# Graph attention score passes: five identity products on TensorE ahead of each group's score transposes

## The chip, the cores and the metric

The kernel runs on one core of a Trainium2 chip. Its time is the device time of one execution in microseconds (us), taken without a profiler; the median of three runs stands for it. The profile comes from one further execution under the hardware profiler, which is longer than the timed runs: its span is 4777.7 us.

## The reference, cut to what matters

Two layers over 3125 nodes and 50000 edges. Layer 0 is a weighted neighbour sum with a small MLP and a mixture of experts. Layer 1 begins with a typed graph attention, then a slice attention. The change touches only the scores of the graph attention:

```
K, Q, V = typed linear maps of the node rows
att   = einsum('ehd,ed->eh', k, q.sum(heads)) / sqrt(56)      # edges src -> dst, k from src, q from dst
att_i = the same with src and dst exchanged
att, att_i = softmax over the edges that end in one node
agg   = sum of att * v over those edges, both directions
```

`k` is the K row of one end with a time embedding behind it, `q` the Q row of the other end summed over four heads (56 numbers, also with a time embedding). A softmax over segments needs the maximum of each segment first, so each direction takes a score pass (all scores, and maxima) and a sum pass (exponentials and weighted sums).

## The kernel before, in words

The edges are sorted by the node in which they end and laid out in 416 blocks of 128 slots, each block in one window of 128 nodes. Four blocks are a group (U = 4), 104 groups are a pass (NG = 104). For each direction `o` there is `score_*(o)` and then `sum_*(o)`, one function for each engine; all loops are written out, each engine runs its instructions in order, and semaphores tie them together.

A group of a score pass goes as follows.

- **GpSimd** (POOL, L1349) gathers the K and V rows of the group's 512 edges with four indirect DMAs into one of four buffers; SyncE loads the edges' time embeddings beside them (L1311) and writes the V rows out for the sum pass (L1326).
- **ScalarE** (ACT) makes the one-hot matrices of the group: `onehot` with four Abs (L1504) and one Relu (L1506). Its other functions are `turned` and `masks`, which copy the turned one-hots out of PSUM bank 0 (L1514 and L1519), and `scores`, which copies the turned score terms out of bank 1 (L1526) and the scores themselves (L1527). In 26 of the 104 steps of a pass it also clears a tile of the accumulator (`clear`, L1530).
- **TensorE** (PE) has four functions: `turn` transposes the four one-hots into bank 0 (L1441); `queries` fetches the summed Q rows into bank 2 or 3, in turn (L1454, L1457 and L1459); `turn_att` transposes the score terms of the group into bank 1 (L1469); `spread` spreads the scores over the nodes of the window in banks 4 to 7, with a mask (L1478 and L1480, four of each, in two halves).
- **VectorE** (DVE) multiplies the K rows with the query bank (L1393, semaphore `prod`), sums to scores (L1400), splits these into three bf16 terms (L1405 to L1408, semaphore `att` after the last), and takes the maxima of the banks 4 to 7 in two halves (L1380, semaphore `bmr`), one half before and one after the split.

TensorE's order is fixed by the loop at L1484. In step `s` it runs `turn_att(s+1)`, `spread(s)`, `queries(s+3)`, `turn(s+4)`. ScalarE's step has `scores(s+1)`, `clear` in each fourth step, `turned(s+3)`, `onehot(s+4)`, `masks(s+3)`. VectorE's step has the product of group `s+2`, its sums, the first maxima of group `s`, the split of group `s+2`, and the second maxima of group `s`.

The waits that matter here: `turn_att(g)` waits for `att` of group g. `scores(g)` on ScalarE waits for `turn_att(g)`. `turn(g+3)`, which needs bank 0 free, waits for `masks(g+2)`, the last thing of ScalarE's step. `queries(g)` waits for the product of group g-2, since this frees the query bank. The second half of `spread(g)` waits for the second maxima of group g-1.

`identb` is a bf16 identity of 128x128.

Of the kernel before, what the change touches and what calls it, by code (L numbers as in the profile page):

```python
# [15 lines left out]
P = 128  # L16
# [9 lines left out]
NG = NB // U  # L26
# [24 lines left out]
def build(nc, A, out):  # L51
    ctx = ExitStack()
    with ctx:
# [3 lines left out]
        def sem(name):  # L57
            if name not in sems:
                sems[name] = ctx.enter_context(nc.semaphore(name))
            return sems[name]  # L60

        def sb(name, shape, dt=F32):
            return ctx.enter_context(nc.sbuf_tensor(name, shape, dt))
# [28 lines left out]
        identb = sb("identb", [P, P], BF16)  # L92
# [33 lines left out]
        PS = [PSA[:, 512 * k:512 * (k + 1)] for k in range(8)]  # L126
# [39 lines left out]
        def loads_of(eng, ap_row, maxv, etype):  # L166
            _, vals = nc.values_load_multi_w_load_instructions(
                ap_row, engines=[etype], min_val=0, max_val=maxv,
                skip_runtime_bounds_check_because="clamped when the table was computed")
            return vals  # L170
# [1127 lines left out]
        def halves(x):  # L1298
            return x.bitcast(BF16).rearrange("p (j two) -> p j two", two=2)[:, :, 1]
# [53 lines left out]
        def score_vector(ve, o):  # L1353
# [67 lines left out]
            ins.then_inc(sem("pass_set"), 1)  # L1421
            ve.drain()

        OT2 = [PS[s][:, 0:U * P // 2].bitcast(BF16) for s in range(2)]

        def transposes(pe, s):
            for u in range(U):
                ins = pe.transpose(OT2[s % 2][:, u * P:(u + 1) * P], halves(OH[s][:, u, :]), identb[:, :])  # L1428
            return ins
# [4 lines left out]
        def score_tensor(pe, o):  # L1434
            def turn(g):
                G = o * NG + g
                pe.wait_ge(sem("oh"), G + 1)
                if g:
                    pe.wait_ge(sem("ot"), 2 * G)
                for u in range(U):  # L1440
                    ins = pe.transpose(OHP[:, u * P:(u + 1) * P], OHB[g % SL][:, u, :], identb[:, :])  # L1441
                ins.then_inc(sem("ohT"), 1)

            def queries(g):
                G, s = o * NG + g, g % SL
                if G == 0:
                    pe.wait_ge(sem("kv_tab"), 32)
                ws = loads_of(pe, win[o][0:1, g * U:(g + 1) * U], W - 1, ET.PE)
                pe.wait_ge(sem("ot"), 2 * G + 1)
                pe.wait_ge(sem(f"edges{s}"), 16 * (3 * o * (NG // SL) + g // SL + 1))  # L1450
                if g >= 2:
                    pe.wait_ge(sem("prod"), G - 1)
                q = PS[2 + g % 2][:, 0:U * 64].rearrange("p (u c) -> p u c", c=64)
                pe.matmul(PS[2 + g % 2][:, 0:U * 64], ZB, identb[:, :].unsqueeze(1).to_broadcast([P, U * 64 // P, P]),  # L1454
                          start=True, stop=False, skip_group_check=True)
                for u in range(U):
                    pe.matmul(q[:, u, 0:DK], OTF[g % 2][:, u, :], QS[:, ds(ws[u], 1), :].rearrange("p t d -> p (t d)"),  # L1457
                              start=False, stop=False, skip_group_check=True)
                pe.matmul(q[:, :, DK - TD:DK], ident[:, :], KVR[s][:, :, KV + 2 * TD:ROW],  # L1459
                          start=False, stop=True, skip_group_check=True).then_inc(sem("q"), 1)  # L1460

            def turn_att(g):
                G = o * NG + g
                pe.wait_ge(sem("att"), G + 1)
                if g:
                    pe.wait_ge(sem("tb"), 2 * G - 1)
                b = BF[g % 2].rearrange("p k n -> p (k n)").bitcast(BF16).rearrange("p (r x) -> p r x", x=2 * H1)
                for h in range(H1):
                    ins = pe.transpose(ATP[0:NR, h * P:(h + 1) * P], b[:, :, 2 * h + 1], identb[:, :])  # L1469
                ins.then_inc(sem("att_t"), 1)  # L1470

            def spread(g):
                G = o * NG + g
                pe.wait_ge(sem("tb"), 2 * G + 1)
                for u in range(U):
                    if u % 2 == 0 and g:
                        pe.wait_ge(sem("bmr"), 2 * (G - 1) + u // 2 + 1)
                    pe.matmul(PS[4 + u], identb[:, :], NEG[g % SL][:, u, :].unsqueeze(1).to_broadcast([P, H1, P]),  # L1478
                              start=True, stop=False, skip_group_check=True)
                    ins = pe.matmul(PS[4 + u], SEL[:, u, :], ATB[g % 2], start=False, stop=True, skip_group_check=True)  # L1480
                    if u % 2:
                        ins.then_inc(sem("bm"), 1)

            for step in range(-4, NG):  # L1484
                if 0 <= step + 1 < NG:
                    turn_att(step + 1)
                if step >= 0:
                    spread(step)
                if 0 <= step + 3 < NG:
                    queries(step + 3)  # L1490
                if step + 4 < NG:
                    turn(step + 4)
# [168 lines left out]
        def sum_scalar(act, o):  # L1661
            def copies(g):
                G = o * NG + g
                act.wait_ge(sem("oh2T"), G + 1)
                if g >= 2:
                    act.wait_ge(sem("m"), G - 1)
                act.activation(OT[g % 2].rearrange("p u n -> p (u n)"), OT2[g % 2], ACT.Copy).then_inc(sem("ot2"), 1)

# [796 lines left out]
        @block.tensor  # L2465
        def _(pe):
            rank_tensor(pe, 0)
            rank_tensor(pe, 1)
            place_tensor(pe, "t", OHt.rearrange("p t g -> p (t g)"), T1)
            l0_tensor(pe)  # L2470
            mlp_tensor(pe)
            route_tensor(pe)
            experts_tensor(pe)
            kvq_tensor(pe)
            for o in range(2):
                score_tensor(pe, o)
                sum_tensor(pe, o)
            slice_prep_tensor(pe)
            turn_types(pe)
            proj_tensor(pe)  # L2480
            gamma_tensor(pe)
            slices_tensor(pe)
            tokens_tensor(pe)
            final_tensor(pe)
# [63 lines left out]
```

## Time and profile before

| | us |
|---|---|
| median of three timed runs | 3957.93 (3956.56 to 3957.97) |
| span of the profiled execution, its own time | 4777.7 |
| score pass, first direction (2260.1 to 2972.3 of the span) | 712.2 |
| score pass, second direction (3339.3 to 4037.7) | 698.4 |

Busy over the whole profiled span: PE 2872.2 us (60%), DVE 2426.9 (51%), ACT 1720.4 (36%), POOL 2723.8 (57%). Times in the rows below are in us from the start of the span. "Granted clock" is the share of TensorE's full 2.4 GHz that its throttle let through: 1.00 or 0.50 (1.2 GHz), and values between the two are means over a stretch. Under the profiler the program takes 819.8 us longer than without it, so a stall seen in the rows need not be in the timed runs.

### The profile page before, as it was taken

What the parts mean: (1) busy time and instruction counts of PE and PEld (TensorE: products, weight loads), DVE (VectorE), ACT (ScalarE), POOL (GpSimd) and SP (SyncE); (2) the same over time, 40 slices, a digit from 0 to 9 for tenths busy, and PEclk for the clock granted to TensorE, in tenths of its full rate; (3) what the DMA queues carried; (4) which work ended last, traced back from release to release, by engine and by line L of the source; (5) the groups of instructions that cost most, each with busy time, mean ns of one, the idle gap of its engine ahead of it and who ended that gap; (6) DMA issues with size and microseconds to landing.
All of it is one profiled execution on the core that took longest, in us unless ns stands there. A gap on an engine that the chain in (4) does not pass through costs nothing.

```text
span 4777.7 us, 52094 instructions
## 1 busy us (share of the span) xinstructions
PE 2872.2 (60%) x13590; PEld 1938.9 (41%) x13692; DVE 2426.9 (51%) x4965; ACT 1720.4 (36%) x4345; POOL 2723.8 (57%) x2661
## 2 busy tenths in 40 slices
PE   3200025555533239367677777997777776997588
PEld 1000013333332126223444444887444444886445
DVE  7444444544421001433667677566677777566353
ACT  2232300000011002222455554786555554885451
POOL 5676756666645740466555554788555553555551
PEclk6555557767665569767777777999777777998799
DMA  4343356333414224267766667687777666665300
GB/s 143 113 172 126 143 111 231 89 89 91 98 57 165 97 89 148 68 200 212 216 199 208 200 200 184 177 213 184 205 202 209 201 202 166 160 173 149 110 1 27
DMA packets 767484, 720.00 MB, mean 151 GB/s; under 512 B 389089, under 2 KB 661163, under 8 KB 767068
## 3 DMA queue, kind: packets, MB, share of 16 engines
q1 hardware_dynamic: 645116, 399.08, 29.2%
q0 software_dynamic: 115136, 314.24, 22.4%
q10 hardware_dynamic: 6944, 3.34, 0.2%
q8 instruction: 119, 1.95, 0.2%
q14 instruction: 169, 1.38, 0.1%
HBM read 482.09 MB, written 243.22 MB: 152 GB/s over the span
## 4 chain that ended last, share of the span: by engine, by line
PE 22%; another core or an unknown queue 17%; DVE 16%; issue 12%; ACT 9%; DVEq 4%; POOL 2%; ACTq 2%; DMA 1%; SPq 1%; POOLq 0%
DVE META L1380 5%; DVE BIGR L605 3%; ACT AR L1674 3%; DVE AR L1400 3%; PE ps L1657 2%; PE ps L933 2%; PE ps L944 2%; ACT AR L1676 2%; DVE AR L596 2%; DVEq L1396 2%; PE ps L1480 1%; PE ps L1478 1%; ACTq L1675 1%; PE ps L1428 1%
## 5 line engine op out<-in xcount | busy, mean ns | idle before, releaser
L1349 POOL DMA_INDIRECT AR<-kv_tab,META x832 | 793.7, 954 | 620.8 <-DVE AR L1393 363.1
L1380 DVE TENSOR_REDUCE META<-ps 128x8 f32<-128x1024 f32 x416 | 508.5, 1223 | 186.3 <-remote 94.2
L493 POOL DMA_INDIRECT rec_dst<-AR,slot_e x400 | 403.3, 1008 | 229.1 <-issue 171.0
L625 PE MATMUL ps<-AR 128*128 128x256 f32 x832 | 318.2, 550 | 345.4 <-DVE AR L596 156.4
L579 POOL DMA_INDIRECT AR<-xn_tab,META x416 | 398.6, 958 | 206.8 <-issue 139.0
L1618 POOL TENSOR_TENSOR AR<-AR 128x896 f32<-128x896 f32 x208 | 351.4, 1689 | 246.1 <-ACT AR L1683 241.6
L1583 DVE TENSOR_TENSOR BIGR<-BIGR,ps 128x260 f32 x832 | 354.3, 426 | 217.4 <-PE ps L1657 131.1
L1478 PE MATMUL ps<-AR,identb 128*128 128x512 bf16 x832 | 403.8, 485 | 79.1 <-issue 55.2
L1657 PE MATMUL ps<-AR 128*128 128x260 f32 x1664 | 413.9, 392 | 2.1 <-POOL AR L1618 2.0
L625 PEld LDWEIGHTS ps<-AR 128*128 128x128 f32 x832 | 219.7, 277 | 445.1 <-issue 214.9
L1526 ACT ACTIVATE AR<-ps 12x512 bf16<-12x512 bf16 x208 | 122.1, 587 | 671.8 <-remote 469.9
L521 POOL DMA_INDIRECT rec_src<-AR,slot_e x290 | 286.6, 988 | 97.5 <-issue 93.1
L1480 PE MATMUL ps<-AR 128*128 128x512 bf16 x730 | 340.9, 467 | 0.0
L605 DVE TENSOR_TENSOR BIGR<-BIGR,ps 128x256 f32 x416 | 174.8, 420 | 311.3 <-remote 151.4
L1393 DVE TENSOR_TENSOR AR<-AR,ps 128x896 f32<-128x896 f32 x208 | 225.2, 1083 | 196.8 <-remote 174.1
L1657 PEld LDWEIGHTS ps<-AR 128*128 128x128 f32 x1664 | 302.0, 192 | 41.1 <-POOL AR L1618 3.3
L1457 PEld LDWEIGHTS ps<-QS,AR 128*128 128x128 f32 x1664 | 271.0, 247 | 19.8 <-issue 12.4
L1457 PE MATMUL ps<-QS,AR 128*128 x1664 | 278.2, 325 | 0.0
L1674 ACT ACTIVATE AR<-iota,META 128x128 f32<-128x128 f32 x832 | 263.4, 390 | 28.3 <-DVE AR L1420 28.3
L1504 ACT ACTIVATE AR<-iota,META 128x128 f32<-128x128 f32 x832 | 262.3, 385 | 24.6 <-DVE AR L1370 24.6
L749 ACT ACTIVATE AR<-ps 128x256 f32<-128x256 f32 x25 | 9.6, 383 | 686.0 <-PE ps L706 663.2
L1400 DVE TENSOR_REDUCE AR<-AR 128x16 f32<-128x896 f32 x208 | 225.9, 1086 | 34.3 <-issue 33.5
(430 smaller groups left out, 5624.0 us busy)
## 6 DMA issues: line engine op xcount, KB each, us to landing
v_dst<-AR SPq DMA_DIRECT2D x104, 384.0 KB
AR<-v_dst SPq DMA_DIRECT2D x104, 384.0 KB
v_src<-AR SPq DMA_DIRECT2D x104, 384.0 KB
AR<-v_src SPq DMA_DIRECT2D x104, 384.0 KB
AR<-in_W_qvk SPq DMA_DIRECT2D x44, 608.0 KB
rec_raw<-AR SPq DMA_DIRECT2D x40, 640.0 KB
AR<-rec_dst SPq DMA_DIRECT2D x104, 192.0 KB
AR<-rec_src SPq DMA_DIRECT2D x104, 192.0 KB
```

What stands on the lines that cost most here:

```text
L493: pool.indirect_dma_start(rec_tab[0], bass.IndirectOffsetOnAxis(ap=slot_e[0][:, c * CC + k:c * CC + k + 1].bitcast(U32), axis=0), RD[s][0] ...
L579: pool.indirect_dma_start(GA[s][:, u, :], None, xn_tab, bass.IndirectOffsetOnAxis(ap=META[0][:, g * U + u, 0:1].bitcast(U32), axis=0)).the ...
L625: ins = pe.matmul(l0_ps(s, u), OW[s][:, u, :], GA[s][:, u, :], start=True, stop=True)
L1349: pool.indirect_dma_start(KVR[s][:, u, 0:KV], None, kv_tab, bass.IndirectOffsetOnAxis(ap=META[o][:, g * U + u, 0:1].bitcast(U32), axis=0)) ...
L1380: ve.tensor_reduce(BMALL[o][:, g * U + 2 * half:g * U + 2 * half + 2, :].rearrange("p b h -> p (b h)"), PSA[:, 2048 + 1024 * half:3072 + 1 ...
L1400: ve.tensor_reduce(x, PRD.rearrange("p u (h d) -> p (u h) d", d=DK), AX.X, ALU.add)
L1457: pe.matmul(q[:, u, 0:DK], OTF[g % 2][:, u, :], QS[:, ds(ws[u], 1), :].rearrange("p t d -> p (t d)"), start=False, stop=False, skip_group_ ...
L1478: pe.matmul(PS[4 + u], identb[:, :], NEG[g % SL][:, u, :].unsqueeze(1).to_broadcast([P, H1, P]), start=True, stop=False, skip_group_check= ...
L1480: ins = pe.matmul(PS[4 + u], SEL[:, u, :], ATB[g % 2], start=False, stop=True, skip_group_check=True)
L1583: ve.tensor_tensor(a, a, PS[4 + u][:, 0:SROW], ALU.add).then_inc(sem("add"), 1)
L1657: pe.matmul(PS[4 + u][:, 0:SROW], OH[s][:, u, :], VB[s][:, u, :], start=True, stop=True).then_inc(sem("sum"), 1)
L1674: act.activation(DIST2[g % 2][:, u, :], iota1[:, :], ACT.Abs, scale=-1.0, bias=META[o][:, g * U + u, 1:2])
```

## The change

At the head of TensorE's step stands a new wait and five matrix products of `identb` with itself, repeated to 512 columns. They are written to the query bank that `queries(step + 3)` fills later in the same step; this first overwrites the bank (`start=True`). The wait is for the product of group `step + 1`, the one that reads this bank last. It happens in the steps 0 to 100 of each pass, that is 202 times, and adds 1010 matrix products.

```
@@ score passes, TensorE @@
+        def warm(pe, bank, width, times):
+            for _ in range(times):
+                pe.matmul(bank[:, 0:width], identb[:, :], identb[:, :].unsqueeze(1).to_broadcast([P, width // P, P]),
+                          start=True, stop=True, skip_group_check=True)
...
             for step in range(-4, NG):
+                if 1 <= step + 1 < NG and step + 3 < NG:
+                    pe.wait_ge(sem("prod"), o * NG + step + 2)
+                    warm(pe, PS[2 + (step + 3) % 2], 512, 5)
                 if 0 <= step + 1 < NG:
                     turn_att(step + 1)
```

## Rows read from the trace of the kernel before

**Rows 1.** The page: granted clock of TensorE in 40 equal slices of the span.

```profile
PEclk6555557767665569767777777999777777998799
```

**Rows 2.** Stretches: both score passes, then one sum pass; columns as named in the first line.

```profile
core 0: us, PE busy (x) PEld busy (x) DVE busy (x) ACT busy (x) POOL busy (x), PEclk, DMA share, GB/s
2260.10:2972.30 712.20, 521.54 (x2722) 318.72 (x2771) 496.56 (x718) 362.04 (x948) 390.16 (x409) 0.75 0.69 203
3339.30:4037.70 698.40, 509.38 (x2718) 311.75 (x2769) 496.79 (x718) 362.02 (x948) 380.94 (x402) 0.77 0.72 201
3003.40:3318.00 314.60, 307.28 (x2043) 274.02 (x2042) 192.19 (x513) 251.39 (x704) 275.72 (x208) 1.00 0.77 201
```

**Rows 3.** Timeline of one group without a stall: start, duration, engine, line.

```profile
2618.69 1.23 DVE L1380 TENSOR_REDUCE META<-ps 128x8 f32<-128x1024 f32 x1
2619.01 0.39 PE L1441 MATMUL ps<-identb,AR 128*128 128x128 bf16 x4
2619.32 0.40 PE L1469 MATMUL ps<-identb,AR 128*12 128x128 bf16 x4
2619.76 0.59 ACT L1526 ACTIVATE AR<-ps 12x512 bf16<-12x512 bf16 x1 [1.39 <-PE ps L1469]
2619.83 1.08 DVE L1393 TENSOR_TENSOR AR<-AR,ps 128x896 f32<-128x896 f32 x1
...
2620.10 0.38 PE L1478 MATMUL ps<-AR,identb 128*128 128x512 bf16 x1
2620.32 0.38 PE L1480 MATMUL ps<-AR 128*128 128x512 bf16 x1
2620.36 0.57 ACT L1514 ACTIVATE AR<-ps 128x512 f32<-128x512 bf16 x1
2620.82 0.96 POOL L1349 DMA_INDIRECT AR<-kv_tab,META  x1 [0.30 <-issue]
2620.84 1.26 ACT L1504 ACTIVATE AR<-iota,META 128x128 f32<-128x128 f32 x4
...
2622.17 0.63 ACT L1506 ACTIVATE AR<-AR 128x512 bf16<-128x512 f32 x1
2622.34 0.45 PE L1459 MATMUL ps<-AR,ident 128*128 128x128 f32 x2
2622.71 0.58 ACT L1519 ACTIVATE AR<-ps 128x512 bf16<-128x512 bf16 x1
2623.43 0.38 PE L1441 MATMUL ps<-identb,AR 128*128 128x128 bf16 x4 [0.65 <-ACT AR L1519]
2623.70 0.18 DVE L1408 TENSOR_TENSOR AR<-AR 128x16 bf16<-128x16 f32 x1
2623.80 1.22 DVE L1380 TENSOR_REDUCE META<-ps 128x8 f32<-128x1024 f32 x1
2623.94 0.40 PE L1469 MATMUL ps<-identb,AR 128*12 128x128 bf16 x4
```

**Rows 4.** The instructions of L1530: times run, duration in ns min/median/max, first and last start.

```profile
L1530 ACT ACTIVATE BIGR<-ones x52: 401/401/403, 2284.3 to 4031.5; 128x260 f32<-128x260 f32 x52
```

**Rows 5.** Stretches without a stall, columns as in rows 2: clock and TensorE's busy time.

```profile
2617.70:2621.10 3.40, 3.40 (x27) 2.35 (x26) 3.17 (x7) 2.01 (x6) 1.24 (x2) 1.00 0.82 272
2965.90:2969.30 3.40, 2.83 (x18) 1.87 (x17) 3.17 (x4) 1.82 (x5) 0.00 (x0) 1.00 0.25 81
```

**Rows 6.** A stretch at the low clock, columns as in rows 2.

```profile
2600.60:2604.00 3.40, 3.18 (x11) 1.26 (x11) 3.17 (x4) 2.82 (x8) 2.74 (x3) 0.50 0.60 168
```

**Rows 7.** Timeline around a stall: low clock before, and low clock again behind it.

```profile
2602.69 0.63 PE L1478 MATMUL ps<-AR,identb 128*128 128x512 bf16 x1
2603.11 0.63 PE L1480 MATMUL ps<-AR 128*128 128x512 bf16 x1
...
2608.09 1.22 DVE L1380 TENSOR_REDUCE META<-ps 128x8 f32<-128x1024 f32 x1 [2.77 <-issue]
2609.72 0.59 ACT L1526 ACTIVATE AR<-ps 12x512 bf16<-12x512 bf16 x1 [5.09 <-remote]
2611.14 1.86 PE L1457 MATMUL ps<-QS,AR 128*128 x8
```

## The prediction

> **What bounds the kernel now.** I read the page's slices first. TensorE's granted clock is 9 tenths or more only in the two short stretches where it is also busiest, and 6 to 7 tenths in most of the rest [rows 1]. Then I set the four passes of the graph attention side by side. A score pass takes 712.2 or 698.4 us at a mean clock of 0.75 to 0.77, a sum pass some 315 us at 1.00 [rows 2]. So the score passes are 1410.6 us of the profiled span of 4777.7 us, 6.8 us for each of 208 groups, and none of the four engines is busy all of it. This is the place that the change touches, and the low clock there is what it could cure.
>
> Next I read the timeline of a group, and there are two kinds. In a group without a stall VectorE is never idle: from the second maxima of one group (2618.69) to those of the next (2623.80) are 5.11 us, filled by the product, the sums, two maxima and the split [rows 3]. I call its period 5.10 us. GpSimd issues a gather every 0.96 + 0.30 us, four of which are 5.04 us, so it is close behind [rows 3]. In the other kind something holds the core for about 3 us: VectorE begins its maxima 2.77 us late with nothing named, ScalarE its copy after 5.09 us idle [rows 7]. At 5.10 us each, the 208 groups would take 1061 us, so stalls make up 350 us of the two passes. The profiled execution is 819.8 us longer than the timed runs. I take it that the stalls belong mostly to the profiler's execution, and that the timed kernel runs its score passes near 5.10 us a group. It is an assumption, and two of the rivals drop it.
>
> **What the low clock costs now.** At the low clock [rows 6] the wide products of `spread` start 0.42 us apart and the eight of L1457 take 1.86 us [rows 7]; at the high clock the wide ones start 0.22 us apart [rows 3], half of it. In the groups without a stall the clock is at its high level [rows 5] although TensorE is busy for only 2.83 of 3.40 us. So without stalls the kernel keeps the high clock by itself, and even right after a stall, where it is low, TensorE sits behind VectorE's 5.10 us by little. What the change can buy back is therefore near nothing.
>
> The Trainium skill speaks for the change: "TensorE: Matmul & The Clock Gate", section "Why this matters for your kernels", advises to leave no long idle gaps between bursts of matmuls, since the clock then falls to half. The trace agrees that the clock is low beside the stalls and high away from them; what filling would bring if the rule decided here is the third rival.
>
> **What the change adds, step by step.**
>
> *Products.* Five bf16 products of 512 columns. The same shape is L1478 and L1480, which start 2620.32 - 2620.10 = 0.22 us apart at the high clock; over the eight of a group it is 0.215. Five are 1.08 us. At the low clock they start 0.42 us apart [rows 7], and five are 2.1 us.
>
> *The wait.* It is for the product of group g that `turn_att(g)` needs anyway through `att`, 3.0 us later: L1393 ends at 2620.91, L1408 at 2623.88 [rows 3]. The wait by itself holds nothing that `turn_att` would not hold. I cost it at 0; between 0 and one semaphore instruction a group, which is under 0.1 us.
>
> *Is TensorE's idle time the cover?* By its busy time, yes: the group's own work is 3.02 us from 2619.32 to 2622.34, then L1459's 0.45 and L1441's 0.31 (2619.01 to 2619.32), at most 3.8 us of 5.10 [rows 3]. With 1.08 more it is 4.9. But the idle time lies in the wrong place. TensorE idles before `turn`, since bank 0 is not free until ScalarE's last copy (L1441 waited 0.65 us for L1519). The new products stand behind `turn` and ahead of `turn_att`, where hardly 0.30 us is idle (2623.43 + 0.31 to 2623.94, and that is the wait for `att`).
>
> *The loop that they lengthen.* `turn_att` starts ScalarE's step, ScalarE's step ends with `masks`, `masks` frees bank 0 for `turn`, and `turn` stands ahead of the next `turn_att` on TensorE. Its parts from start to start [rows 3]: L1469 to L1526 0.44; L1526 to L1514 0.60; L1514 to L1504 0.48; L1504 to L1506 1.33; L1506 to L1519 0.54; L1519 to L1441 0.72; L1441 to the next instruction of TensorE 0.31. The sum is 4.42 us. Now it is hidden behind VectorE's 5.10, with 0.68 to spare. With the products between `turn` and `turn_att` it is 4.42 + 1.08 = 5.50 us, and it takes the lead. A clear (L1530) of 0.40 us stands in it in every fourth step [rows 4], which was hidden as well: 0.10 a group more, 5.60 us.
>
> *Sum.* 5.60 - 5.10 = 0.50 us for each of 202 groups is 101 us. Nothing hides it: VectorE then waits for the first half of `spread`, and the gathers' 5.04 us and what the DMA needs fit in with room. Everything outside the score passes stays. Bounds of this term: if only what exceeds VectorE's period counts and no clear adds, 0.40 x 202 = 81 us; if the wait and the first product's start add 0.1, 121 us.
>
> The sum against the profiled execution is 4777.7 + 101 = 4879, with more if products fall into the low clock beside a stall. Carried to the timed runs, which lack 819.8 us of it, it is **3957.9 + 101 = 4059 us**.
>
> **The rivals.**
>
> *1. Cover from elsewhere.* Score groups of the timed runs already take longer than 5.10 us because of DMA. For it: the 16 DMA engines are busy for 0.69 of 712.2 us [rows 2], that is 4.7 us of each group, and the gathers' issue takes 5.04. Against: groups at 5.10 occur while gathers run. At a true period of 5.4 the price is 0.2 x 202 = 40 us, at 5.6 nothing: 3958 to 3998, say 3975.
>
> *2. The stalls are in the timed runs too.* Then ScalarE's copy, late behind `turn_att` by the stall, is on the same loop, and the stall leaves the low clock, so that the five cost 2.1 in one group and 1.08 in the next, with 0.2 to 0.3 us of slack in each: (2.1 + 1.08 - 0.5)/2 = 1.3 us a group at the most, 0.7 if the clock stays up. 202 groups give 140 to 275 us: 4100 to 4230. Against: then the 819.8 us must come from the rest of the program alone.
>
> *3. Faster: the clock decides.* If the timed kernel runs its score groups at 1.2 GHz, TensorE's group is at least 3.8 + 8 x 0.21 for `spread` + 0.8 for L1457 (1.86 less what half of that leaves, with its own 0.1 of start) = 6.3 us and is itself the bound. Were that so in half of the groups, a mean group takes 5.7 us. With the five it takes 5.6, and the kernel is 20 us faster; were it so in all, 6.3 to 5.6 saves 140 us: 3818 to 3938, say 3900. It decides only where the low clock is found in more than 0.5/1.2 = 42% of the groups. For it: the mean of 0.75, which is half the time at the low level. Against: the low level stands beside the stalls, and the group right behind one is VectorE's again.
>
> **How the numbers follow.** The loop through ScalarE, 4059 us with its own range 4035 to 4085, gets 0.58. The covered case (3975) gets 0.17, the stalls that stay (4100 to 4230) 0.12, the clock (3900) 0.13. About 0.2% (8 us) is what a measurement of this kernel can tell from no change. The clock's case is faster by more than that: with a little for luck, faster 0.13. Of the covered case somewhat over half falls within 8 us: same 0.10. The rest is slower: 0.77. For 8 in 10 I leave out the faster case below 3950 and the upper part of the stalls' above 4125.
>
> **What the changed profile would show.** If the step is right: five new products between L1441 and L1469 in each group; L1469 late behind L1408 by 0.5 us or more; groups without a stall at 5.5 to 5.6 us; VectorE idle before its first maxima, with TensorE's spread as what ended it; ScalarE idle for some 2 us ahead of its L1526 and hardly elsewhere. The granted clock of the score passes would rise from 0.75 without their time falling. Rival 1 shows groups no longer than before, L1469 still released by VectorE. Rival 3 shows shorter score passes. I am wrong if `turn` ends well before `att` in the undisturbed groups, for then the five lie in idle time.

## The result and the profile after

The changed kernel takes 4046.01 us (median of four, 4042.42 to 4049.05), the kernel before 3957.95 (median of four, 3956.56 to 3958.45): 88 us slower, ratio 1.0223 with a 95% interval of 1.0211 to 1.0235. The forecast was 4059 us.

The profiled execution of the changed kernel has a span of 4044.2 us and a device time of 4045.93, in the middle of the other three. A profiled execution is therefore not bound to be longer, and the 4777.7 us of the profile before need another reason than the profiler. The runs below show one. They come in two conditions: in one the kernel before takes 3957 us, in the other it takes 4742 to 4772 us (medians on three chips), with the stalls of [rows 7] in its traces. I call the second the condition with stalls. Each price below is against the kernel before on the same chip and in the same condition. Two executions that fit neither condition, one of the kernel before (4372.71 us) and one of a changed kernel (6208.72 us), are left out of the ratios, which can differ in the fourth place from those of the medians.

The page of the kernel after: span and instructions, then the granted clock in 40 slices.

```profile
span 4044.2 us, 54114 instructions
...
PEclk6555557777776996889999989998999999997798
```

Stretches of the kernel after, columns as in [rows 2]: its two score passes, then its first sum pass.

```profile
1805.50:2378.30 572.80, 496.11 (x3221) 295.86 (x3271) 488.80 (x718) 361.34 (x947) 389.08 (x409) 0.99 0.86 253
2745.00:3317.10 572.10, 495.69 (x3221) 295.80 (x3270) 489.75 (x718) 361.38 (x947) 380.77 (x403) 0.99 0.89 246
...
2410.30:2725.00 314.70, 307.47 (x2044) 274.69 (x2043) 192.25 (x513) 251.51 (x704) 275.54 (x208) 1.00 0.77 201
```

The clock of the score passes is 0.99, and each takes 572 us. [Rows 2] have 0.75 and 0.77, but from the condition with stalls, so the two clocks alone do not say what the products did to it. From product to product there are 103 steps in a pass, 5.56 us each. VectorE is busy for 488.8 of 572.8 us: it waits. The sum pass is as before, 314.7 us.

Timeline of one group of the kernel after, which answers to [rows 3]. Lines have moved: L1427 is the new product; L1475, L1535, L1523, L1513, L1515, L1528 and L1447 are what L1469, L1526, L1514, L1504, L1506, L1519 and L1441 were.

```profile
2100.84 0.40 PE L1475 MATMUL ps<-identb,AR 128*12 128x128 bf16 x4
...
2101.28 0.59 ACT L1535 ACTIVATE AR<-ps 12x512 bf16<-12x512 bf16 x1 [1.98 <-PE ps L1475]
...
2101.88 0.57 ACT L1523 ACTIVATE AR<-ps 128x512 f32<-128x512 bf16 x1
...
2102.26 1.23 DVE L1380 TENSOR_REDUCE META<-ps 128x8 f32<-128x1024 f32 x1 [0.48 <-PE ps L1486]
...
2102.36 1.26 ACT L1513 ACTIVATE AR<-iota,META 128x128 f32<-128x128 f32 x4
...
2103.69 0.63 ACT L1515 ACTIVATE AR<-AR 128x512 bf16<-128x512 f32 x1
2103.72 0.18 DVE L1408 TENSOR_TENSOR AR<-AR 128x16 bf16<-128x16 f32 x1
...
2104.22 0.58 ACT L1528 ACTIVATE AR<-ps 128x512 bf16<-128x512 bf16 x1
2104.95 0.38 PE L1447 MATMUL ps<-identb,AR 128*128 128x128 bf16 x4 [0.64 <-ACT AR L1528]
...
2105.17 1.24 PE L1427 MATMUL ps<-identb 128*128 128x512 bf16 x5
...
2106.34 0.40 PE L1475 MATMUL ps<-identb,AR 128*12 128x128 bf16 x4
```

Read it as a loop, from L1475 to L1475. To ScalarE's first copy 0.44 us, then 0.60, 0.48, 1.33, 0.53 along ScalarE's step, 0.73 to `turn`, 0.22 to the first product, and 1.17 through the products to the next `turn_att`. (A start here is that of the first instruction of each kind.) The sum is 5.50 us, and the group lasts 5.50 us. From `turn` to the instruction behind it are 0.22 us, less than the 0.31 before the change, so the new wait holds nothing. `att` (L1408, done at 2103.90) has been ready for 2.4 us when `turn_att` starts at 2106.34: VectorE no longer sets the pace. ScalarE waits 1.98 us for `turn_att`, VectorE 0.48 us for the spread scores.

The same over all groups, from the page's costliest groups: ScalarE's wait for `turn_att` in both passes.

```profile
L1535 ACT ACTIVATE AR<-ps 12x512 bf16<-12x512 bf16 x208 | 121.9, 586 | 415.4 <-PE ps L1475 415.4
```

That is 2.0 us for each of 208 groups. A group with a clear shows the second part, here ScalarE's timeline with and then without it:

```profile
2084.49 0.59 ACT L1535 ACTIVATE AR<-ps 12x512 bf16<-12x512 bf16 x1 [1.98 <-PE ps L1475]
2084.98 0.20 ACT L1536 ACTIVATE AR<-AR 128x16 f32<-128x16 f32 x1
2085.09 0.40 ACT L1539 ACTIVATE BIGR<-ones 128x260 f32<-128x260 f32 x1
2085.39 0.57 ACT L1523 ACTIVATE AR<-ps 128x512 f32<-128x512 bf16 x1
...
2090.29 0.59 ACT L1535 ACTIVATE AR<-ps 12x512 bf16<-12x512 bf16 x1 [1.98 <-PE ps L1475]
2090.79 0.20 ACT L1536 ACTIVATE AR<-AR 128x16 f32<-128x16 f32 x1
2090.89 0.57 ACT L1523 ACTIVATE AR<-ps 128x512 f32<-128x512 bf16 x1
```

From L1535 to L1523 are 0.90 us with the clear and 0.60 without: the copies and the clear overlap by 0.1, and the clear costs 0.30 of its 0.40.

### The profile page after: what moved, and what is told of

The parts are those of the page before. It is cut to its first block, busy times and chain, and to the rows that moved or that the text cites. A ratio compares the mean times of both kernels' runs of the same rounds, so it can differ in the third digit from the quotient of the medians.

```text
span 4044.2 us, 54114 instructions
## 1 busy us (share of the span) xinstructions
PE 2752.9 (68%) x14600; PEld 1872.6 (46%) x14702; DVE 2419.8 (60%) x4965; ACT 1719.1 (43%) x4345; POOL 2730.1 (68%) x2661
## 4 chain that ended last, share of the span: by engine, by line
PE 30%; ACT 20%; issue 15%; DVE 5%; POOL 5%; ACTq 4%; DMA 4%; DVEq 1%; SPq 1%; POOLq 1%
PE ps L625 6%; ACT AR L1513 6%; PE ps L1427 5%; ACT AR L1683 5%; ACT AR L1528 3%; PE ps L944 3%; ACT AR L1685 3%; ACT AR L1523 2%; ACTq L1514 2%; PE ps L1447 2%; ACTq L1684 2%; PE ps L1434 2%; PE ps L1475 2%; PE ps L933 1%; DMA BIGR<-in_L_ffn_w 1%
## 5 line engine op out<-in xcount | busy, mean ns | idle before, releaser
L625 PE MATMUL ps<-AR 128*128 128x256 f32 x832 | 303.6, 530 | 287.5 <-issue 216.4
L625 PEld LDWEIGHTS ps<-AR 128*128 128x128 f32 x832 | 210.5, 265 | 381.5 <-issue 340.1
L1484 PE MATMUL ps<-AR,identb 128*128 128x512 bf16 x832 | 320.0, 385 | 5.9 <-DVE META L1380 0.5
L1666 PEld LDWEIGHTS ps<-AR 128*128 128x128 f32 x1664 | 302.6, 192 | 40.4 <-POOL AR L1627 3.2
L1535 ACT ACTIVATE AR<-ps 12x512 bf16<-12x512 bf16 x208 | 121.9, 586 | 415.4 <-PE ps L1475 415.4
L1486 PE MATMUL ps<-AR 128*128 128x512 bf16 x730 | 279.0, 382 | 0.0
L1513 ACT ACTIVATE AR<-iota,META 128x128 f32<-128x128 f32 x832 | 262.2, 385 | 24.6 <-DVE AR L1370 24.6
L1427 PE MATMUL ps<-identb 128*128 128x512 bf16 x1010 | 252.8, 382 | 0.0
```

What stands on the lines that cost most here:

```text
L625: ins = pe.matmul(l0_ps(s, u), OW[s][:, u, :], GA[s][:, u, :], start=True, stop=True)
L1427: pe.matmul(bank[:, 0:width], identb[:, :], identb[:, :].unsqueeze(1).to_broadcast([P, width // P, P]), start=True, stop=True, skip_group_ ...
L1513: act.activation(DIST[:, u, :], iota1[:, :], ACT.Abs, scale=-1.0, bias=META[o][:, g * U + u, 1:2])
L1666: pe.matmul(PS[4 + u][:, 0:SROW], OH[s][:, u, :], VB[s][:, u, :], start=True, stop=True).then_inc(sem("sum"), 1)
```

## The experiments

The theory is the loop: the products stand between `turn` and the next `turn_att`, and that chain through ScalarE becomes longer than VectorE's 5.10 us. Its rivals here are that five more products cost what they cost wherever they stand, that the new wait costs, and that the clock decides.

**The place.** The wait and the five products are moved to just before `queries`. The kernel ran in both conditions; the run without stalls, the later one, is shown first.

```diff
             for step in range(-4, NG):
-                if 1 <= step + 1 < NG and step + 3 < NG:
-                    pe.wait_ge(sem("prod"), o * NG + step + 2)
-                    warm(pe, PS[2 + (step + 3) % 2], 512, 5)
                 if 0 <= step + 1 < NG:
                     turn_att(step + 1)
                 if step >= 0:
                     spread(step)
+                if 1 <= step + 1 < NG and step + 3 < NG:
+                    pe.wait_ge(sem("prod"), o * NG + step + 2)
+                    warm(pe, PS[2 + (step + 3) % 2], 512, 5)
                 if 0 <= step + 3 < NG:
                     queries(step + 3)
```

> The five products between spread and queries once more, for a run where the kernel before takes 3958 us. Loop theory there: TensorE's chain is 4.4 + 0.31 = 4.7 us, under VectorE's 5.10: 3958 to 3973 us. Rival, TensorE's plain time or traffic: 4046 us. Where stalls of 3 us come in every other group and the kernel before takes some 4742 us: 10 us more than before, as measured.

Measured, without stalls: 3961.07 us against 3956.59 for the kernel before, ratio 1.0011 (1.0002 to 1.0020). The same 1010 products and the same 202 waits cost 88 us in one place and 4 us in the other, as the loop had it (3958 to 3973) and not its rival (4046). Its timeline, one group:

```profile
2033.37 1.22 DVE L1380 TENSOR_REDUCE META<-ps 128x8 f32<-128x1024 f32 x1
2033.52 0.41 PE L1475 MATMUL ps<-identb,AR 128*12 128x128 bf16 x4 [0.33 <-DVE AR L1408]
...
2035.59 1.24 PE L1427 MATMUL ps<-identb 128*128 128x512 bf16 x5
...
2036.90 0.58 ACT L1528 ACTIVATE AR<-ps 128x512 bf16<-128x512 bf16 x1
...
2037.90 0.39 PE L1447 MATMUL ps<-identb,AR 128*128 128x128 bf16 x4
...
2038.47 1.22 DVE L1380 TENSOR_REDUCE META<-ps 128x8 f32<-128x1024 f32 x1
2038.61 0.40 PE L1475 MATMUL ps<-identb,AR 128*12 128x128 bf16 x4 [0.33 <-DVE AR L1408]
```

The group lasts 5.10 us from maxima to maxima, and `turn_att` is released by VectorE's L1408. Here `turn` (2037.90) comes behind TensorE's own queue, 0.4 us after bank 0 was free, and there are still 0.33 us to spare. Its two score passes:

```profile
1805.50:2339.70 534.20, 492.35 (x3268) 303.58 (x3267) 489.89 (x718) 361.10 (x946) 388.97 (x409) 0.98 0.92 271
2706.20:3232.20 526.00, 491.21 (x3273) 302.39 (x3271) 488.91 (x717) 361.64 (x948) 381.00 (x403) 0.99 0.95 268
```

Together 1060.2 us, against 1144.9 for the changed kernel. The difference, 84.7 us, is all but 1 us of that between the two spans (4044.2 and 3958.5). So the whole loss lies in the score passes and in the place of the products. Clock and TensorE's busy time are alike in both (0.98 to 0.99; 983.6 and 991.8 us), which leaves neither the clock nor plain TensorE time as the cause. The moved kernel also tells against the case in which the clock decides: its passes run at the high clock, nearly all their groups last 5.10 us, and it isn't faster than before.

The kernel before has no trace without stalls, but its executions beside the moved kernel have a mean clock each. The median is 0.833, against 0.839 for the moved kernel. If the whole difference lies in the score passes, which are 1060 of 3958 us, then those of the kernel before run at about 0.96, by my estimate; at 0.76 its mean would have been some 0.78. So without stalls there was hardly any clock to win back.

The same kernel with stalls:

> The same wait and the same five products, moved from the head of the step to between spread and queries, so that they no longer stand between turn and the next turn_att. Loop theory: TensorE's chain from turn_att to turn is 3.3 + 1.08 = 4.4 us and ScalarE's 4.1, then 0.31 for turn, together 4.7 under VectorE's 5.10: 3958 us, up to 15 more. Rival, plain TensorE time or traffic (five more products cost what they cost wherever they stand): 4046 us. Rival, the clock: 3900 us, since the clock is high and the loop is not lengthened.

4753.25 us against 4741.99, ratio 1.0026 (1.0016 to 1.0036), 11 us. The values expected were for 3958 us and are not tested by it.

**The wait alone**, with stalls: the change without its five products.

```diff
                 if 1 <= step + 1 < NG and step + 3 < NG:
                     pe.wait_ge(sem("prod"), o * NG + step + 2)
-                    warm(pe, PS[2 + (step + 3) % 2], 512, 5)
```

> Only the wait for the product, without the five products. Loop theory: the wait is met 3 us before turn_att's own, so 3958 us, within 8 us of before. Rival, the wait: the time of the changed kernel, about 4046 us, or a good part of it.

4743.93 against 4741.99 us, ratio 1.0001 (0.9990 to 1.0012). No price of the wait shows in this condition. In the other it was not run alone; there the timeline after has products right behind `turn`, 0.22 us after its start.

**The condition with stalls.** The kernel before, unchanged, was profiled twice more, each time for a trace without stalls.

> The kernel before, unchanged, profiled a second time, to see its score passes without the profiler's stalls. Loop theory (the five products lengthen the chain turn, products, turn_att, ScalarE's step, turn): a span near 3956 us, both score passes together about 1058 us, groups of 5.10 us with VectorE never idle, and TensorE's clock at 0.9 to 1.0 in them. Rival, the clock: the clock in these passes is near 0.75 here too, and groups are uneven.

> The kernel before once more, profiled, hoping for an execution without stalls (3957 us). Loop theory: every group of both score passes 5.10 us, VectorE busy all of it, both passes together some 1058 us, and TensorE's clock at 0.9 to 1.0 in them, so that there was nothing for the filler to cure. Rival, the clock: near 0.75 there even without stalls.

Both fell into the condition with stalls: 4742.22 us (ratio 1.0003, 0.9992 to 1.0014) and 4774.14 us (0.9997, 0.9982 to 1.0012). So there is no trace of the kernel before without stalls, and the group of 5.10 us in it, with VectorE never idle, rests on [rows 3] and on the moved kernel. These are the score passes of the first of the two.

```profile
2255.50:2949.90 694.40, 516.14 (x2768) 313.72 (x2767) 493.17 (x717) 361.56 (x948) 388.95 (x409) 0.76 0.71 208
3317.90:4000.00 682.10, 518.02 (x2764) 312.78 (x2765) 493.90 (x718) 361.56 (x948) 379.85 (x402) 0.77 0.76 206
```

The low mean clock of 0.76 belongs to this condition, and so do the 6.7 us a group. The score passes hold less than half of the loss: in the profile before they take 350 us more than in the moved kernel's trace (1410.6 against 1060.2), and the part ahead of them takes 455 us more (2260 against 1805.5). The sum pass has none of it. The runs with stalls were on three chips and those beside the moved kernel without stalls on a fourth, so it stays open whether the condition goes with the chip or with the time, and what the stalls are; no run here tells it.

**The change in that condition.**

> The changed kernel once more. Where the kernel before takes 3958 us: 4046 us. Where it takes some 4742 us, with stalls of about 3 us in every other group of the score passes: loop theory, if a stall lies on the loop turn, products, turn_att, ScalarE's step: 0.45 to 1.3 us a group more, 4830 to 5000 us. Rival, the stall runs beside the products and covers them in every other group: the five cost half or less, 4745 to 4790 us.

4769.19 us against 4744.75, ratio 1.0052 (1.0033 to 1.0070), 24 us. This is the rival's value (4745 to 4790); what the loop theory expected here, 4830 to 5000, is missed. The interval also overlaps that of the moved kernel with stalls (11 us), so in this condition the place of the products is not shown to matter. Its score passes:

```profile
2244.00:2946.40 702.40, 549.50 (x3273) 309.22 (x3271) 494.86 (x718) 361.50 (x947) 388.83 (x409) 0.91 0.70 206
3317.30:4014.10 696.80, 551.40 (x3270) 311.04 (x3270) 495.54 (x718) 361.62 (x948) 379.81 (x402) 0.92 0.73 202
```

The clock rose from 0.76 to 0.91 and the passes did not get shorter: 1399.2 us against 1376.5, the latter from another chip; a second trace of the kernel before with stalls has 1403.2. VectorE's products in the changed kernel, over two groups:

```profile
2559.07 1.09 DVE L1393 TENSOR_TENSOR AR<-AR,ps 128x896 f32<-128x896 f32 x1 [3.00 <-remote]
...
2564.18 1.08 DVE L1393 TENSOR_TENSOR AR<-AR,ps 128x896 f32<-128x896 f32 x1
...
2572.39 1.09 DVE L1393 TENSOR_TENSOR AR<-AR,ps 128x896 f32<-128x896 f32 x1 [1.61 <-remote]
```

One group lasts 5.11 us and the next 8.21, together 13.32 (`remote` stands for a release by another core or an unknown queue). Of the 206 steps of both passes 95 last about 5.10, although the loop with the products needs 5.50, and such a pair has a median of 13.33 us, where the kernel before has 13.30 to 13.45 in its traces with stalls. Two turns of the lengthened loop, 11.0 us at the high clock, fit into that. So what the loop adds disappears in time that the stall takes anyway, in most pairs; where the 24 us lie is not shown.

**The number of products**, three and ten in place of five, at the place of the change.

```diff
-                    warm(pe, PS[2 + (step + 3) % 2], 512, 5)
+                    warm(pe, PS[2 + (step + 3) % 2], 512, 3)      # the other kernel: 10
```

> Three products in place of five, in the place of the change. Loop theory: 4.42 + 3 x 0.215 = 5.07 us, just under VectorE's 5.10; only the groups with a clear (one in four) go over, by about 0.3 us: 3958 + 50 x 0.3 = 3973 us. Rival, cost in proportion to the products: 3958 + 88 x 3/5 = 4011 us.

> Three products at the place of the change. Without stalls, loop theory: 4.42 + 0.65 = 5.07 us, under VectorE's 5.10, over it only in groups with a clear: 3957 + 50 x 0.3 = 3972 us. Rival, in proportion to the products: 4010 us.

> Ten products in place of five, same place. Loop theory where no stalls are: each product beyond the third adds its 0.215 us to each of 202 groups, so 5 more than the changed kernel add 217 us: 4263 us, a group 6.6 us. Where stalls are: 150 to 220 us more than the changed kernel. Rival, TensorE's own busy time is the bound: 3.8 + 2.15 = 5.9 us a group, 4120 us.

> Ten products at the place of the change. Without stalls, loop theory: 5.50 + 5 x 0.215 = 6.6 us a group, 4046 + 217 = 4263 us. Rival, TensorE's busy time as the bound: 3.8 + 2.15 = 5.9 us a group, 4120 us.

All four ran with stalls, so the values expected for 3957 us were not tested. Three cost 6 us (4748.08 against 4741.99, ratio 1.0018, 1.0005 to 1.0030) and 9 us (4781.82 against 4772.39, 1.0027, 1.0009 to 1.0044). Ten cost 100 us (4844.48 against 4744.75, 1.0196, 1.0169 to 1.0223) and 183 us (4955.41 against 4772.39, 1.0387, 1.0354 to 1.0419). On the chip with the 100 us, five cost 24, a quarter, for half the products. So the cost isn't in proportion to the products. It grows faster beyond five, which fits a loop that must first outgrow something else, but in this condition that is the stall and not VectorE's 5.10 us. The size was missed: ten were expected to cost 150 to 220 us more than five, and cost 75 more (4844.48 against 4769.19). On the chip with the 183 us five were not run at this place. Why ten lost 100 us on one chip and 183 on the other stays open. A stretch between two stalls, on the second of these chips, shows the length of the loop with ten:

```profile
2604.69 0.40 PE L1475 MATMUL ps<-identb,AR 128*12 128x128 bf16 x4
...
2606.10 1.23 DVE L1380 TENSOR_REDUCE META<-ps 128x8 f32<-128x1024 f32 x1 [1.87 <-PE ps L1486]
...
2608.79 0.38 PE L1447 MATMUL ps<-identb,AR 128*128 128x128 bf16 x4 [0.64 <-ACT AR L1515]
2609.01 2.32 PE L1427 MATMUL ps<-identb 128*128 128x512 bf16 x10
...
2611.27 0.41 PE L1475 MATMUL ps<-identb,AR 128*12 128x128 bf16 x4
```

From `turn_att` to `turn_att` are 6.58 us, against 5.50 with five: 1.08 us for five products more, 0.216 each, as the loop theory had it (6.6). TensorE's busy time is not the bound, since it waits for ScalarE ahead of `turn` here too.

**The clear**, moved to the end of ScalarE's step in the changed kernel.

```diff
-                if step >= 0 and step % 4 == 0:
-                    clear(step // 4)
                 if step + 3 < NG:
                     turned(step + 3)
                 if step + 4 < NG:
                     onehot(step + 4)
                 if step + 3 < NG:
                     masks(step + 3)
+                if step >= 0 and step % 4 == 0:
+                    clear(step // 4)
```

> The changed kernel with ScalarE's clear (0.40 us, every fourth step) moved from behind scores to the end of its step, behind masks, where it no longer holds bank 0 for turn. Loop theory: the groups with a clear fall from 5.8 us to 5.5: 51 x 0.3 to 0.4 = 15 to 20 us less than the changed kernel, 4028 us where the changed kernel takes 4046. Rival, ScalarE's busy time counts wherever it stands: no change against the changed kernel.

> The changed kernel with ScalarE's clear behind masks. Without stalls, loop theory: the groups with a clear fall from 5.8 to 5.5 us, 4046 - 51 x 0.35 = 4028 us. Rival: 4046 us, since ScalarE does the same work.

Both again with stalls: 4768.33 us against 4744.75 (ratio 1.0053, 1.0035 to 1.0071), where the changed kernel on the same chip had 4769.19; and 4804.68 against 4772.39 (1.0078, 1.0054 to 1.0102), where the changed kernel was not run beside it. No gain shows. Nothing follows for the condition without stalls, where the clear's 0.30 us is read from the timeline only.

## Why the prediction was right, and where it was not

*The step that carried it* was the loop, and it is shown: by the timeline after, part for part, and by the moved products. Forecast were 5.50 us a group and 5.60 with the clears' share; measured are 5.50 and a mean of 5.56.

*The size.* 101 us were forecast, 88 measured. The clear was counted at 0.40 us and costs 0.30, which is 0.025 us a group and 5 us in all. The rest lies in 5.56, a mean over all 206 steps with the faster ones at a pass's start: (5.56 - 5.10) x 202 = 93 us. The last 5 us are in the 5.10, which is a group at its best and not the mean. Outside the score passes the two traces without stalls take 2898.3 and 2899.3 us, which leaves the kernel before some 1057 us for its own two passes, 5.13 a step (an estimate; the moved kernel has 5.19 and 5.11). From 5.13 to 5.56 over 206 steps are 88 us.

*The wait* was costed at 0, and no run or row shows a price of it.

*TensorE's idle time in the wrong place* was the argument against busy time as a cover, and the moved kernel shows it: in the other place the idle time does cover the five. The profile that was forecast is the one that came: groups of 5.5 us, `turn_att` late behind `att`, VectorE waiting for `spread`, ScalarE idle for 2 us ahead of its first copy.

*The clock.* "What the change can buy back is therefore near nothing" holds in both conditions. Without stalls the clock was high already, by the estimate above. With them it rose from 0.76 to 0.91 in the score passes, and the kernel did not become shorter. The third rival falls.

*Where the prediction was wrong:* it took the 819.8 us between span and timed median for the profiler's stalls. The changed kernel was profiled at 4044.2 us and the moved one at 3958.5, without them, and whole series of the kernel before have them. The forecast came out because the runs of both kernels in the result were without stalls, as assumed, but for another reason than the one given. That part is luck: with stalls the same change costs 24 us.

*The second rival* named a condition that exists but was not that of the result, and it had the effect the wrong way round. It expected the stalls to raise the price, to 140 to 275 us; they lowered it to 24. It had put the stall and the products on one chain, one behind the other. (Its 0.7 us a group with the clock up is also short by its own sum: (1.08 + 1.08 - 0.5)/2 is 0.83.) The *first rival*, a cover from elsewhere, is not met without stalls: it needed groups of 5.4 us or more, and in the moved kernel groups run at 5.10 us with the DMA engines busy for 0.92 to 0.95 of the time. With stalls it comes nearest: groups there take 6.7 us already, and the price is small.

## What to carry to other kernels

Idle time of an engine is a cover only for work that is put where the idle time lies. Before adding filler, follow the chain through the other engines from the place of the filler back to itself, sum its starts, and compare with the period: here 4.42 us of 5.10 left room for three products by the sum, not for five (three were not run without stalls). And a low mean clock is no cost by itself; ask first whether the engine that it slows is late for anybody. A profile whose span is far from the timed median may be of another condition, to be cleared up before its idle times are used.

## What the runs showed of the hardware

The same kernel takes 3957 us in some series of runs and 4742 to 4772 us in others, and profiled executions come in both. In the condition with stalls the score passes have a stall of about 3 us in every other group, and all comparisons differ: five products cost 2.2% in the one and 0.5% in the other. In an undisturbed score pass of the changed kernel TensorE was busy for 496 of 573 us at a granted clock of 0.99. bf16 products of 512 columns in a row start 0.216 us apart at the high clock and 0.42 at the low one [rows 7].
